# A graph network's node stage, moved beside the tiles of the layer ahead of it

## The reference

```
edge_index = jnp.stack([src, dst])
# layer 0: (its index pair is (src, dst); messages are summed at dst)
agg = segment_sum(edge_weight[:, None] * x[src], dst)
x   = layernorm(x + relu((x + agg) @ W1 + b1) @ W2 + b2)
# layer 1: (gathers h1 at dst, sums at src)
h1  = x @ lin1_w.T
c   = 0.5 * (cos(edge_weight * pi / 10) + 1)
e   = softplus(edge_attr @ nn_w1.T + nn_b1) - log 2
W   = (softplus(e @ nn_w2.T + nn_b2) - log 2) * c[:, None]
h2  = h1 + segment_sum(W * h1[dst], src)
out = layernorm(x + h2 @ lin2_w.T + lin2_b)
```

## Time and profile before

| | |
|---|---|
| median of 3 runs | 8774.11 us (8772.1 to 8775.9) |
| the profiled execution | 8796.3 us, its span 8794.7 us |
| PE / DVE / ACT / POOL busy | 5927.9 / 5851.1 / 3465.1 / 6213.8 us |
| mean granted TensorE clock | 0.738 of full speed |

### The profile page before, as it was taken

The page is one execution under the profiler, slowest core; times in us unless marked ns, Lnnn a source line. Parts: engine busy times, 40 slices in busy tenths (PEclk is TensorE's granted clock), DMA queues, the critical chain, the costliest instruction groups (busy, mean ns, idle before and its releaser), DMA issues. The chain is left out here.

```text
span 8794.7 us, 201979 instructions
## 1 busy us (share of the span) xinstructions
PE 5927.9 (67%) x35386; PEld 4731.0 (54%) x35658; DVE 5851.1 (67%) x17865; ACT 3465.1 (39%) x6782; POOL 6213.8 (71%) x6560
## 2 busy tenths in 40 slices
PE   5676676667676676666655556666767666666787
PEld 3444444444444444444444445666666666666676
DVE  6666666666666666665655556777777777777776
ACT  3434344443444444444544443334444343443302
POOL 6777777777777777775377777777777777777710
PEclk7766676666776767667755557888888888888897
DMA  5444454444444445444444446666666666666676
GB/s 165 154 152 153 150 155 151 154 151 152 154 153 153 153 153 153 153 153 148 143 133 134 135 131 191 212 213 213 213 215 213 212 215 211 215 215 211 215 238 203
DMA packets 805506, 1537.47 MB, mean 175 GB/s; under 512 B 193406, under 2 KB 207156, under 8 KB 804963
## 3 DMA queue, kind: packets, MB, share of 16 engines
q1 hardware_dynamic: 595415, 1097.64, 38.8%
q0 software_dynamic: 209712, 436.16, 16.9%
q10 hardware_dynamic: 348, 3.33, 0.1%
HBM read 971.97 MB, written 564.58 MB: 175 GB/s over the span
## 5 line engine op out<-in xcount | busy, mean ns | idle before, releaser
L1353 POOL DMA_INDIRECT sorted_messages<-rows,sidx x3224 | 3115.5, 966 | 1153.4 <-issue 946.9
L516 POOL DMA_INDIRECT xg<-x_rows,gidx x3224 | 3050.4, 946 | 1032.8 <-issue 858.9
L584 PE MATMUL bank<-attr,nn 128*128 128x512 f32 x1612 | 1484.7, 1075 | 191.0 <-DMA attr<-attr_cols 181.6
L573 PE MATMUL bank<-onehot,xg 128*128 128x42 f32 x6448 | 945.1, 303 | 845.5 <-DMA xg<-x_rows,gidx 838.1
L1281 PE MATMUL bank<-hot,block_rows 128*128 128x128 f32 x8256 | 1390.0, 344 | 30.0 <-DVE hot L1435 29.9
L1281 PEld LDWEIGHTS bank<-hot,block_rows 128*128 128x128 f32 x8256 | 1342.8, 258 | 55.7 <-issue 17.8
L573 PEld LDWEIGHTS bank<-onehot,xg 128*128 128x128 f32 x6448 | 877.1, 212 | 882.0 <-DMA xg<-x_rows,gidx 874.4
L1251 PE MATMUL bank<-w_nn2T,e_hid 128*128 128x128 f32 x6448 | 1041.9, 314 | 293.1 <-DMA e_hid<-hidden 285.2
L1251 PEld LDWEIGHTS bank<-w_nn2T,e_hid 128*128 128x128 f32 x6448 | 1008.2, 226 | 250.3 <-DMA e_hid<-hidden 217.2
L465 ACT ACTIVATE soft<-bank 128x512 f32<-128x512 f32 x808 | 475.3, 588 | 1332.8 <-PE bank L584 1332.5
L1262 PE MATMUL bank<-h1w,ohT 128*128 128x128 bf16 x3224 | 337.9, 268 | 982.1 <-DVE ohT L1382 982.1
(11 more groups left out here) (220 smaller groups left out, 8235.4 us busy)
## 6 DMA issues: line engine op xcount, KB each, us to landing
block_rows<-sorted_messages SPq DMA_DIRECT2D x346, 792.0 KB
hidden<-hid SPq DMA_DIRECT2D x404, 512.0 KB
e_hid<-hidden SPq DMA_DIRECT2D x403, 512.0 KB
sorted_messages<-zero SPq DMA_DIRECT2D x403, 264.0 KB
dstb<-dst SPq DMA_DIRECT2D x403, 256.0 KB
attr<-attr_cols SPq DMA_DIRECT2D x403, 204.0 KB
xg<-x_rows,gidx POOLq DMA_INDIRECT x3224
sorted_messages<-rows,sidx POOLq DMA_INDIRECT x3224
```

Of the source, the lines that this page charges most:

```text
L516: pool.indirect_dma_start(xg[b][s][:, :], None, x_rows, bass.IndirectOffsetOnAxis(ap=gidx[b][s // HALF][:, s % HALF:s % HALF + 1], axis=0) ...
L573: nc.tensor.matmul(bank[0][:, 0:WIN], xg[b][s][:, :], onehot[:, s, :], start=(s == 0), stop=(s == SUB - 1)).then_inc(summed[b], 1)
L584: nc.tensor.matmul(bank[2 + h][:, :], nn1[:, :], attr[:, h, :], start=True, stop=True).then_inc(z1_set, 1)
L1353: pool.indirect_dma_start(table, bass.IndirectOffsetOnAxis(ap=sidx[b][h][:, s:s + 1], axis=0), rows[b][h][:, s, :], None).then_inc(landed[ ...
```

## The change

The separate block is gone. `layer0_nodes` is replaced by a function `stage(k, n)` on each engine, k from 0 to 6, for slot n, and `in_segments` calls it behind every second tile: a loop body now holds 14 tiles and the seven stages of one slot. There are 28 slots (7 in each part). Which unit a slot works on comes from `node_table`, which `find_units` computes on DVE ahead of the first tile from the tiles' lowest nodes: a unit is given to a slot only once all its sums are complete, and a slot for which none is ready works on an unused unit behind the table. What the 28 slots have not done, `rest_of_units` does behind the last tile, one unit after another. A slot has one buffer of each kind and PSUM bank 5 alone. The root of the variance becomes ACT's Ln and Exp. The diff below is cut: its stages are SP's, ACT's and PE's, in that order.

```diff
-CHUNK = 13
+CHUNK = 10
...
+STAGES = 7
+SEG = 2 * STAGES
...
+def segments(first, past_last):
+
+    even = first + first % 2
+    return even, (min(past_last, T - 1) - even) // SEG
...
+                def rest_of_units(engine, stage):
+
+                    with engine.Fori(0, units_remaining(engine)) as r:
+                        for k in range(STAGES):
+                            stage(k, r + NODE_SLOTS)
...
+                            if k == 0:
+                                unit_at(sp, unit, n)
+                                at = sp.snap(unit, min_val=0, max_val=NPAD)
+                                sp.wait_ge(node_parts_set, n + 1)
+                                sp.dma_start(node_rows[:, :, :], unit_rows(x_rows, at)).then_inc(xr_in, 16)
...
+                        def stage(k, n):
+                            if k == 0:
+                                act.wait_ge(node_up, n + 1)
+                                nc.scalar.activation(node_cols[:, :].rearrange("f (g p) -> f g p", g=G), bank[5][:, :].rearrange("f (p g) -> f g p", g=G),
+                                                     ACT.Relu, bias=b1c[:, 0:1]).then_inc(node_hid, 1)
+                            if k == 2:
+                                act.wait_ge(node_norm, n * NODE_STEPS + (1 + 2 * G))
+                                nc.scalar.activation(node_rstd[:, :], node_mv[:, :, 1], ACT.Ln, bias=eps[:, 0:1]).then_inc(node_log, 1)
+                                act.wait_ge(node_log, n + 1)
+                                nc.scalar.activation(node_rstd[:, :], node_rstd[:, :], ACT.Exp, scale=-0.5).then_inc(node_rstd_set, 1)
+                            if k == 4:
+                                act.wait_ge(node_turned, n + 1)
+                                nc.scalar.activation(node_cols[:, :], bank[5][:, :], ACT.Copy).then_inc(node_x1T, 1)
+                            if k == 5:
+                                act.wait_ge(node_lin, n + 1)
+                                act.wait_ge(x1_st, 16 * (n + 2))
+                                nc.scalar.activation(node_rows[:, :, :], bank[5][:, :].rearrange("p (g d) -> p g d", g=G), ACT.Copy)
+                                act.wait_ge(parts_st, 16 * (n + 1))
+                                nc.scalar.activation(node_parts[:, :, 0, :], bank[5][:, :].rearrange("p (g d) -> p g d", g=G), ACT.Copy).then_inc(node_high, 1)
+                            if k == 6:
+                                unit_at(act, unit, n)
+                                at = act.snap(unit, min_val=0, max_val=NPAD)
+                                act.wait_ge(node_h1T_made, n + 1)
+                                nc.scalar.activation(aggT[:, ds(at, UNIT)].rearrange("f (p g) -> f g p", g=G),
+                                                     bank[5][:, :].rearrange("f (g p) -> f g p", g=G), ACT.Copy).then_inc(node_h1T, 1)
...
-                        in_pairs(act, 0, T - 1, tile)
+                        for q, first, past_last in parts:
+                            in_segments(act, first, min(past_last, T - 1), SLOT_OF_PART[q], tile, stage)
...
+                        rest_of_units(act, stage)
+                            if k == 0:
+                                unit_at(pe, unit, n)
...
+                                nc.tensor.matmul(bank[5][:, :], w_sb["W1"][:, :], aggT[:, ds(at, UNIT)], start=True, stop=True).then_inc(node_up, 1)
...
+                            if k == 5:
+                                pe.wait_ge(node_x1T, n + 1)
+                                for g in range(G):
+                                    ins = nc.tensor.matmul(bank[5][:, g * P:g * P + P], node_cols[:, g * P:g * P + P], w_sb["lin1T"][:, :],
+                                                           start=True, stop=True)
+                                ins.then_inc(node_lin, 1)
+                            if k == 6:
+                                pe.wait_ge(node_high, n + 1)
+                                nc.tensor.matmul(bank[5][:, :], w_sb["lin1T"][:, :], node_cols[:, :], start=True, stop=True).then_inc(node_h1T_made, 1)
...
+def in_segments(engine, first, past_last, slot, tile, stage):
+    even, count = segments(first, past_last)
+    if first % 2:
+        with engine.Fori(first, first + 1) as t:
+            tile(t, 1)
+    with engine.Fori(0, count) as c:
+        for k in range(STAGES):
+            for b in range(2):
+                tile(c * SEG + (even + 2 * k + b), b)
+            stage(k, c + slot)
+    in_pairs(engine, even + count * SEG, past_last, tile)
```

More of the change, by code:

```diff
@@ L51 @@
 HIST_STEPS = 4
+STAGES = 7
+SEG = 2 * STAGES
+NODE_STEPS = 1 + 3 * G
+PART_TILES = [(q * PT, min((q + 1) * PT, T)) for q in range(PARTS)]
+def segments(first, past_last):
+    even = first + first % 2
+    return even, (min(past_last, T - 1) - even) // SEG
+SEGMENTS = [segments(*p)[1] for p in PART_TILES]
+SLOT_OF_PART = [sum(SEGMENTS[:q]) for q in range(PARTS)]
+NODE_SLOTS = sum(SEGMENTS)
+TILES_BEFORE = [segments(*p)[0] + c * SEG + 2 for p in PART_TILES for c in range(segments(*p)[1])]
 assert SUMMING % 2 == 0 and TABLE_TILES % 2 == 0
@@ L445, in _ @@
                                 row = sp.snap(end, min_val=0, max_val=TABROWS - BLOCK)
-                                sp.dma_start(sorted_d[k][ds(row, BLOCK), :].rearrange("(p g) d -> p (g d)", p=P), zero[:, :]).then_inc(blocks_cleared, 16)
+                                sp.dma_start(table[ds(row, BLOCK), :].rearrange("(p g) d -> p (g d)", p=P), zero[:, :]).then_inc(blocks_cleared, 16)
+                            in_segments(sp, first, past_last, SLOT_OF_PART[q], tile, stage)
                         store_hidden(T)
@@ L495, in _ @@
+                        act.sem_inc(node_h1T, 1)
                         copy_indices(0, 0)
-                        in_pairs(act, 0, T - 1, tile)
+                        for q, first, past_last in parts:
+                            in_segments(act, first, min(past_last, T - 1), SLOT_OF_PART[q], tile, stage)
                         softplus_1(T - 1, (T - 1) % 2)
@@ L522, in _ @@
                         in_pairs(pool, 0, T, tile)
+                        for b in range(2):
+                            for h in range(2):
+                                for k in range(HALF):
+                                    row = 40 + 8 * b + 4 * h + k
+                                    prime(pool, spare[row:row + 1, :], landed[b][h], zero)
+                        for b in range(2):
+                            for h in range(2):
+                                pool.wait_ge(landed[b][h], 16 * HALF)
@@ L584, in tile @@
                                     nc.tensor.matmul(bank[2 + h][:, :], nn1[:, :], attr[:, h, :], start=True, stop=True).then_inc(z1_set, 1)
-                            in_pairs(pe, first, past_last, tile)
+                            pe.wait_ge(plan, PLAN_STEPS * (q + 1))
+                            in_segments(pe, first, past_last, SLOT_OF_PART[q], tile, stage)
+                        wait_apart(pe, flushed, jobs.number() + 2, pe_passed)
+                        rest_of_units(pe, stage)
                     @block.vector
@@ L720, in tile @@
                                 hidden(t, 1)
-                            in_pairs(dve, first, past_last, tile)
+                            in_segments(dve, first, past_last, SLOT_OF_PART[q], tile, stage)
                         end = jobs.number()
@@ L818, in in_pairs @@
     even = first + first % 2
-    with engine.Fori(0, (past_last - even) // 2) as c:
-        for b in range(2):
-            tile(c * 2 + (even + b), b)
+    if past_last - even >= 2:
+        with engine.Fori(0, (past_last - even) // 2) as c:
+            for b in range(2):
+                tile(c * 2 + (even + b), b)
     if past_last % 2:
@@ L1585 @@
     w = np.concatenate([w, np.zeros(pad, w.dtype)])
-    xp = np.zeros((NPAD, D), x.dtype)
+    xp = np.zeros((NPAD + UNIT, D), x.dtype)
     xp[:N] = x
```

314 lines of the change are left out of this document (150 added, 164 removed).

## The result

The changed kernel takes 8960.1 us (median of 4 runs, 8947.1 to 8962.9) against 8773.1 us (4 runs, 8768.7 to 8775.9): ratio 1.0211 with a 95% interval of [1.0197, 1.0224], **187 us slower**. Its profiled execution took 8957.7 us, with a span of 8956.1 us and a mean granted clock of 0.742 (before 0.738).

What follows compares the result with a forecast made beforehand. POOL's gathers, one every 1.25 us, were taken to bound layer 0. From the profiled 8796.3 us: - 135.6 + 252 + 28 + 2.5 = 8943, a median of 8921 us; range 8790 to 9020.

Steps and rivals of the forecast that it cites:

- The cost: what the stages hold up: Layer 0: ACT's index copies wait behind stages 0, 4, 5 and 6, making gathers late; 9.0 us a slot, 252 us.
- The room: Layer 0: z1 ends 0.6 to 2.2 us ahead of the first gather of tile t + 2; taken as 1.4 us.
- The heads of the parts: At each part's start PE is behind after the plan, so POOL waits 7 us; in four parts 28 us.
- The rival of the loops that no longer fit: Jumps back of the 14-tile body fetch code ahead of an index copy; 2.0 us each, 56 us, 8977 us; chance 0.17.
- The prediction's sign for it: Listed under wrong: an extra wait of 2 us or more only behind stage 6, with code packets by the hundred.
- its own sign: Listed under right: some 112 POOL waits of 2 to 3 us for ACT's index copy, behind stages 0, 4, 5, 6.
- The gain: Between the layers: the node stage shrinks to two leftover units, first scatter from 4305.9 to 4170.3; 135.6 us saved.
- Small ones: Ahead of the first tile: find_units on DVE taken as 2 us, extra prologue operations 0.5 us; 2.5 us together.
- The clock rival: Chip grants z1 the upper clock level, so z1 ends 1.9 us sooner; 8663 us; copies on time, chance 0.15.

Runs made afterwards that it cites:

- e1: The changed kernel with ACT's index copy for tile t+2 written ahead of the stage and of the jump back: 8738.1 us, ratio 0.9962 to the kernel before.
- e3: The changed kernel with PE's stage written ahead of the tile's z1 matmuls instead of behind them: 8729.5 us, ratio 0.9948 to the kernel before.
- e4: The kernel before, nothing moved, with ACT's, PE's and DVE's layer 0 loops written out to 14 tiles a body instead of 2: 8772.9 us, ratio 0.9999.
- e7: The changed kernel with loop bodies of 28 tiles on all four engines, 8 jumps back instead of 24: 8866.8 us, ratio 1.0106 to the kernel before.
- e9: The changed kernel with 28-tile loop bodies on ACT alone, 14-tile bodies on SP, PE and DVE: 8894.3 us, ratio 1.0119 to the kernel before.
- e10: The changed kernel with 28-tile loop bodies on SP, PE and DVE, ACT keeping 14 tiles: 8959.7 us, ratio 1.0190 to the kernel before.
- e5: The changed kernel with ACT's index copy ahead of the stage and PE's stage ahead of z1: 8660.7 us, ratio 0.9870 to the kernel before.
- e8: The kernel of e5 with SP's four clears written ahead of the store of the last hidden tile: 8671.0 us, ratio 0.9865 to the kernel before.
- e11: The kernel of e5 with each part's clear of its last blocks issued at that part's end: 8653.6 us, ratio 0.9863 to the kernel before.
- e2: The changed kernel with ACT's index copy still behind the stage but ahead of the jump back: 8926.3 us, ratio 1.0173 to the kernel before.

## Why the prediction was right, and where it was not

Slower, by the mechanism named, at 8960 us where 8921 was given (187 us more than before where 147 were forecast), inside the range. But what happened is the forecast's sum together with its first rival, and the number owes something to luck. By its steps:

- **The cost: what the stages hold up.** Right in its places: late copies behind stages 0, 4, 5 and 6, none behind 1, 2 and 3, and e1 and e3, which each take away one link of the chain, each take away three quarters of it. Wrong in size: 252 us for 28 slots; measured 35.5 us behind stage 0 without the heads (24 slots, 1.5 us each), 1.3 behind stage 4, 1.85 behind stage 5 and some 1.3 behind stage 6 without a jump (1.1 to 2.0), 6.0 us a slot and not 9.0, **about 165 us**. At the place shown for stage 5 the room (964.45 - 963.08 = 1.37 us) is what was taken, PE's part is 1.47 us past z1 (taken 1.6) and ACT's 1.20 (1.3); at the place for stage 6 the release is 0.88 us (991.86 to 992.74), as taken. What was mis-sized most is the index copy: 0.55 us with 0.35 of idle time ahead came from a place where it waited for nothing; behind the evacuations it follows without a gap and ends 0.09 us behind them in stages 0 and 5 and 0.16 in stage 4, on the mean of 28 places each. At 112 places that is some 50 of the 87 us. The room was 1.2 us at stage 4, 1.5 at stage 5 and 2.05 at stage 6 on the mean (taken 1.4), which is some 18 us more at stage 6. The rest was not traced.
- **The heads of the parts**, 28 us: measured 10.9, 8.3, 7.6 and 7.7 us, less 1.5 each for the ordinary lateness: 28.5 us. This term is right.
- **The rival of the loops that no longer fit** was not a rival but part of the same run. It was left out of the sum, and priced at 2.0 us a jump, with 3.5 as the upper end, at 28 jumps; it is 4.1 to 5.2 us at 24 jumps (at the end of a part the loop falls through), some 114 us. The bound failed because it took the 4.6 us of a load of x for the longest fetch and let 1.1 us of it pass beside ACT's evacuation; the idle time behind that evacuation is 3.95 to 5.37 us by itself. That the copy is hit twice (stage late, then fetch) is why this case pays and e4 does not. The prediction's sign for it, an extra wait only behind stage 6 and code packets by the hundred, showed; the prediction had put it among the signs of being wrong, beside its own sign, late copies behind the four stages, which showed as well. The Trainium skill (Runtime: NRT & Kernel Launch, section on instruction fetch mechanics) says that a taken branch outside the current window waits for a fetch; e7, e9 and e10 agree, and e4 adds that it costs only where nothing covers it.
- So 280 us were predicted for stages and heads, and 309 measured with the jumps: **the sum came out near because 87 us too much for the stages and nothing for the jumps, some 114 us, nearly cancel**. With the stages as predicted and the jumps as measured the forecast would have been 8921 + 114 = 9035 us, beyond its range.
- **The gain**: gap 66.5 us predicted, 72.6 measured. The first unit's load was issued 24.5 us behind the last gather and not 18.6, so its residual add came at 27.6 and not 23.2 us (+4.4); from there the unit took 12.4 us and not 11.3, the second 17.8 and not 16.4, barrier and loads 14.7 and not 15.6. Two units were left over, as counted. 129.5 us were saved, 135.6 predicted.
- **Small ones**, 2.5 us: the first gather came 2.4 us sooner, not later; why is open.
- **The clock rival** did not show: 0.72 granted beside the tiles against 0.70, and z1 still 3.76 us in the rows above; over all slots, z1 ahead of a stage takes 3.6 to 3.7 us on the mean, whichever stage, as before. Its number, 8663 us for copies on time, is what e5 reached by another way, the order of the streams: 8660.7.
- The profiled execution of the kernel before was 22 us over its median. In part this is POOL's rows being a few ns longer (last section), which is why the profiled executions differ by 161 us and the medians by 187.

## What to carry to other kernels

Work put beside the engine that bounds a kernel cost nothing here by its share of time; it cost by what stands behind it in program order. Before a stage with waits is put into a stream, write whatever the bound engine waits for ahead of it (here two moves, 300 us), and on the producer's side put the stage ahead of the long work it need not wait for. A longer loop body (14 tiles here, where 2 needed none) brought a fetch at its jump: put the jump where the engine has lead, or make the body longer still, so that there are fewer jumps. And behind a queue's instructions stand their bytes: in e8, issuing bulk transfers earlier did not free the way for the small load behind them; spreading them over the run did (e11).

## What the hardware showed that I had not expected

- A jump back of the 14-tile body holds ACT 3.95 to 5.37 us and DVE 3.3 to 4.1 us in the changed kernel. The same code run straight on holds ACT not at all in e9, though it too comes through the code queue (308 packets there, 341 in the change).
- The second queue that carries code, q8, went from 31 packets (0.51 MB) to 174 (2.85 MB) in e7 and 173 in e10, the kernels with 28 tiles in the bodies of SP, PE and DVE, without a cost that the time shows. Whose code it is, the trace does not say.
- POOL's indirect DMAs have two paces: scatters 0.966 us on the mean in the profiled executions of before, e2, e3 and e10, 0.962 to 0.963 in the others, which is 4096 to 4097 against 4084 to 4088 us from the first to the last scatter. Ten us of a difference between two profiled executions can be this alone. It seems to go by execution and not by kernel, since the four executions at the longer pace are each the longest of their kernel; but no kernel was profiled at both. What sets the pace is open.
